# The rest of the folded queries made by TensorE and taken by ScalarE, the folded pieces ahead of the scores

## The reference

```python
q_c_lat = _linear(x, d_q_w, d_q_b); kv_c = _linear(x, d_kv_w, d_kv_b)
q_c = _linear(q_c_lat, u_q_w, u_q_b); k_c = _linear(kv_c, u_k_w, u_k_b)
q_r, k_r = _rope(_linear(q_c_lat, qr_w, qr_b)), _rope(_linear(kv_c, qr_w, qr_b))
q, k = concatenate([q_c, q_r]), concatenate([k_c, k_r])
scores = einsum('bhqd,bhkd->bhqk', q, k) / sqrt(192)
ctx = einsum('bhqk,bhkd->bqhd', softmax(scores), v)
out = _linear(ctx, out_w, out_b)
```

## Time and profile before

| | us |
|---|---|
| median of 3 runs | 2483.41 |
| lowest and highest | 2482.87, 2486.58 |
| profiled execution, span from first to last instruction | 2481.1 |
| TensorE busy | 2204.9 (89%) |
| VectorE busy | 2144.0 (86%) |
| ScalarE busy | 1862.6 (75%) |
| GpSimd busy | 1073.9 (43%) |

### The profile page before, as it was taken

How to read it: one execution, slowest core, us unless ns; L and a number is a source line. 1 busy time by engine, 2 the same in 40 slices (tenths; PEclk the granted TensorE clock), 3 DMA queues, 4 the chain that set the end, 5 groups by cost and what they waited for, 6 DMA issues and landing times.

```text
span 2481.1 us, 50682 instructions
## 1 busy us (share of the span) xinstructions
PE 2204.9 (89%) x18456; PEld 1581.5 (64%) x18544; DVE 2144.0 (86%) x3182; ACT 1862.6 (75%) x2640; POOL 1073.9 (43%) x1480
## 2 busy tenths in 40 slices
PE   4888888869997889999999999999999999988899
PEld 2444444445554567777777777767767777766687
DVE  6888888768896999999999999999999999988522
ACT  4877777747675688888888888888888888877411
POOL 3312112102223575666656656656656656622200
PEclk9999999979998899999999999999999999999899
DMA  3000000050000599999999999999999999999100
GB/s 128 1 2 2 2 2 2 1 115 1 1 1 1 92 182 191 197 188 188 197 190 194 192 192 193 192 189 191 196 191 190 193 194 192 205 192 193 41 17 17
DMA packets 1119318, 300.69 MB, mean 121 GB/s; under 512 B 1107232, under 2 KB 1116416, under 8 KB 1118208
## 3 DMA queue, kind: packets, MB, share of 16 engines
q1 hardware_dynamic: 1116224, 295.21, 68.7%
q10 hardware_dynamic: 2848, 2.23, 0.3%
HBM read 18.45 MB, written 2.10 MB: 8 GB/s over the span
## 4 chain that ended last, share of the span: by engine, by line
DVE 28%; PE 21%; issue 9%; ACT 4%; DMA 4%; SPq 0%; DVEq 0%; ACTq 0%
DVE parts L1651 13%; DVE lows L1635 12%; DMA partsT<-parts 4%; PE psS L1586 3%; PE psOb L1506 3%; PE psS L1489 2%; PE psS L1491 2%; PE psS L1490 2%; ACT parts L1835 2%; PE psOb L1542 1%; PE psOb L1507 1%; ACT prob L1825 1%; PE psOb L1606 1%; PE psPb L1606 1%; DVE rden L1661 1%
## 5 line engine op out<-in xcount | busy, mean ns | idle before, releaser
L1825 ACT ACTIVATE prob<-psS,shift 128x1024 f32<-128x1024 f32 x512 | 574.4, 1122 | 171.0 <-DVE shift L1643 161.2
L1651 DVE TENSOR_TENSOR parts<-prob,parts 128x1024 f16<-128x1024 f32 x512 | 661.0, 1291 | 20.8 <-ACT parts L1835 17.3
L1635 DVE TENSOR_REDUCE lows<-psS 128x1 f32<-128x1024 f32 x512 | 621.9, 1215 | 4.9 <-PE psS L1491 4.7
L1835 ACT CAST parts<-prob 128x1024 f16<-128x1024 f32 x512 | 536.7, 1048 | 21.2 <-DMA partsT<-parts 17.4
L1489 PE MATMUL psS<-k_hi,q_lo 128*128 128x512 f32 x1024 | 449.8, 439 | 100.3 <-ACT prob L1825 93.4
L1506 PEld LDWEIGHTS psOb<-kv,partsT 128*128 128x128 f16 x4096 | 356.7, 97 | 92.1 <-issue 75.7
L1506 PE MATMUL psOb<-kv,partsT 128*128 128x130 f16 x4096 | 396.3, 221 | 13.9 <-DMA partsT<-parts 13.8
L1490 PE MATMUL psS<-k_lo,q_hi 128*128 128x512 f32 x1024 | 407.1, 398 | 0.0
L1491 PE MATMUL psS<-k_hi,q_hi 128*128 128x512 f32 x1024 | 406.9, 397 | 0.0
L1507 PE MATMUL psOb<-kv,partsT 128*128 128x66 f16 x4096 | 386.3, 192 | 0.0
L1507 PEld LDWEIGHTS psOb<-kv,partsT 128*128 128x128 f16 x4096 | 360.1, 98 | 1.0 <-issue 1.0
(11 more groups left out here) (298 smaller groups left out, 4024.2 us busy)
## 6 DMA issues: line engine op xcount, KB each, us to landing
partsT<-parts SPq DMA_TRANSPOSE x512, 4.8
ef<-in_ewT SPq DMA_DIRECT2D x1, 2048.0 KB, 11.1
rf<-in_rwT SPq DMA_DIRECT2D x1, 2048.0 KB, 10.4
outw_s<-in_outwT SPq DMA_DIRECT2D x1, 2048.0 KB, 8.6
trig<-in_trig SPq DMA_DIRECT2D x2, 1024.0 KB, 11.2
out_x<-ot SPq DMA_DIRECT2D x16, 128.0 KB, 1.7
wug<-in_wupT SPq DMA_DIRECT2D x4, 256.0 KB, 3.9
wug<-in_wgateT SPq DMA_DIRECT2D x4, 256.0 KB, 3.7
```

What stands on the lines that cost most here:

```text
L1635: dve.tensor_reduce(lows[:, n % 2, g:g + 1], psS[:, (2 * n + g) % 3, :], AX_X, ALU.min).then_inc(half_min, 1)
L1651: dve.tensor_tensor(parts[:, s, 1, :], prob[:, g, :], parts[:, s, 0, :], ALU.subtract).then_inc(low_done, 1)
L1825: act.activation(prob[:, g, :], psS[:, (2 * n + g) % 3, :], ACT.Exp, bias=shift[:, n % 2:n % 2 + 1], scale=-1.0).then_inc(exp_done, 1)
L1835: act.copy(parts[:, s, 0, :], prob[:, g, :]).then_inc(high_done, 1)
```

## The change

- A tile `negative` of 128x128 in float32r: its latent rows hold minus the identity in the latent columns and zero in the rotary columns. VectorE makes it with two instructions ahead of the first rotation and counts `negated`; TensorE waits for that once, ahead of the loop.
- For heads 1 to 15, VectorE's `rest` goes. Instead TensorE, behind the contexts of the same iteration, waits for `folded` and adds `negative^T q_hi` to the bank psP (`lessen`), counting `lessened`; ScalarE, in the next iteration behind `exponential(n,0)` and ahead of `normalise(n-3)`, waits for `lessened` and writes `q_lo = psP + beta_h` (the new `rest`, counting `rested`).
- TensorE makes the folded piece (piece mod 3 is 2) ahead of `scores(n+1,0)`. The other pieces stay behind the scores.
- Nothing changes for head 0's pieces, for the other engines' orders, or in the waits of `project`.

```diff
--- before.py
+++ after.py
@@ -1330,11 +1330,13 @@
         part = sb(L, "part", [P, D])
         lows = sb(L, "lows", [P, 2, 2])
         shift = sb(L, "shift", [P, 2])
+        negative = sb(L, "negative", [P, P], F32R)
 
         piece_ready, rotated, added_up = sem("b_piece"), sem("b_rotated"), sem("b_added_up")
         round_done, rests_done = sem("b_round"), sem("b_rests")
         keys_summed, keys_rested = sem("b_keys_summed"), sem("b_keys_rested")
         folded, rested = sem("b_folded"), sem("b_rested")
+        negated, lessened = sem("b_negated"), sem("b_lessened")
         score_ready, half_min, shift_ready, exp_done = sem("b_score"), sem("b_half_min"), sem("b_shift"), sem("b_exp")
         high_done, low_done = sem("b_high"), sem("b_low")
         landed = [sem(f"b_landed{s}") for s in range(RING)]
@@ -1461,6 +1463,12 @@
                     pe.matmul(bank, fl2, lat_hi[0:C, cols], start=True, stop=False)
                     pe.matmul(bank, fh2, lat_lo[0:C, cols], start=False, stop=False)
                     pe.matmul(bank, fh2, lat_hi[0:C, cols], start=False, stop=True).then_inc(piece_ready, 1)
+
+            def lessen(head, piece):
+                j = piece // 3
+                pe.wait_ge(folded, 4 * head + j + 1)
+                pe.matmul(psP[:, :], negative[latent, :], q_hi[latent, q_slot(head, j), :], start=False, stop=True,
+                          skip_group_check=True).then_inc(lessened, 1)
 
             def scores(n, g):
                 if n >= TILES:
@@ -1548,13 +1556,19 @@
                 project(0, piece)
             scores(0, 0)
             scores(0, 1)
+            pe.wait_ge(negated, 1)
             for n in range(TILES + 2):
+                piece = piece_at(n) if n < TILES else None
+                if piece is not None and piece % 3 == 2:
+                    project(n // NT + 1, piece)
                 scores(n + 1, 0)
                 scores(n + 1, 1)
-                if n < TILES and piece_at(n) is not None:
-                    project(n // NT + 1, piece_at(n))
+                if piece is not None and piece % 3 < 2:
+                    project(n // NT + 1, piece)
                 context(n - 2, 0)
                 context(n - 2, 1)
+                if piece is not None and piece % 3 == 2:
+                    lessen(n // NT + 1, piece)
                 output(n - LATER)
                 for i in units_at.get(n, ()):
                     spread(i)
@@ -1719,6 +1733,8 @@
                                   ALU.subtract).then_inc(keys_rested, 1)
                 dve.wait_ge(keys_rested, j + 1)
 
+            dve.tensor_scalar(negative[latent, rotary], ident[latent, rotary], 0.0, None, ALU.mult)
+            dve.tensor_scalar(negative[latent, latent], ident[latent, latent], -1.0, None, ALU.mult).then_inc(negated, 1)
             for j in range(NB):
                 rotate(0, 3 * j)
                 rotate(0, 3 * j + 1)
@@ -1735,8 +1751,8 @@
                 low(n, 0)
                 half(n + 1, 1)
                 whole_min(n + 1)
-                if n < TILES and piece_at(n) is not None:
-                    (rotate, rotate, rest)[piece_at(n) % 3](n // NT + 1, piece_at(n))
+                if n < TILES and piece_at(n) is not None and piece_at(n) % 3 < 2:
+                    rotate(n // NT + 1, piece_at(n))
                 invert(n - 2)
                 if n == TILES - 4:
                     scale_signs()
@@ -1802,6 +1818,11 @@
                 act.activation(q_hi[latent, slot, :], piece_bank(head, piece)[latent, :], ACT.Identity,
                                bias=beta_h[latent, 0:1]).then_inc(folded, 1)
 
+            def rest(head, piece):
+                slot = q_slot(head, piece // 3)
+                act.wait_ge(lessened, 4 * (head - 1) + piece // 3 + 1)
+                act.activation(q_lo[latent, slot, :], psP[latent, :], ACT.Identity, bias=beta_h[latent, 0:1]).then_inc(rested, 1)
+
             def round_queries(head, j, halves_scored):
                 act.wait_ge(added_up, sums(head, j) + 1)
                 if halves_scored:
@@ -1878,6 +1899,8 @@
             for n in range(TILES + 3):
                 ahead = n < TILES and n // NT + 1 < NH
                 exponential(n, 0)
+                if 0 < n <= TILES and piece_at(n - 1) is not None and piece_at(n - 1) % 3 == 2:
+                    rest((n - 1) // NT + 1, piece_at(n - 1))
                 normalise(n - 3)
                 take_output(n - LATER - 1)
                 high(n, 0)
```

## The result

| | before | after |
|---|---|---|
| median, us | 2484.72 (4 runs, 2482.87 to 2486.58) | 2569.22 (4 runs, 2567.43 to 2572.24) |
| ratio, 95% interval | | 1.034 (1.0328 to 1.0353) |
| span of the profiled execution, us | 2481.1 | 2570.9 |

The change makes the kernel 3.4% slower, some 85 us. The direction and the main mechanism were forecast, the size was not: +45 us, with an upper end of +75. This is a wrong prediction of the size.

The account below looks back on a forecast made before the run. It took the fixed engine orders in each tile as the limit, with VectorE full where it does a rotation. Losses of 20.8 and 17.9 us, 7.2 for meetings, less 1, gave +45 us: 2528.5 us, range 2510 to 2558.

Parts of the forecast that it names:

- part 3: Folded piece ahead of the scores: TensorE waits for VectorE's rotation, so `half(n+1,0)` comes 1.27 us late, 1.33 with a take.
- a rival of 0.11: Slower by much more: long GpSimd meetings, a late ScalarE rest or a 1.2 GHz TensorE clock; about 2575 us, chance 0.11.
- part 1: Rest leaves VectorE for ScalarE, whose step costs 0.60 us: the rest's period gains 0.62 us without a take, 0.68 with one.
- without a take: Tiles where ScalarE does no `take_output`, 32 of the 60 rest periods: net loss 0.65 us each, 20.8 us.
- meetings: VectorE and GpSimd instructions that overlap and slow each other: 0.12 us in each of 60 places, 7.2 us.
- With a take: Tiles where ScalarE does `take_output`, 28 of the 60 rest periods: net loss 0.64 us each, 17.9 us.
- parts 1 and 4: Part 1 has its own line; the other: VectorE's `low` against GpSimd additions, 0.12 us each, bounds 0 and 0.5.
- the ring: VectorE-ScalarE loop from `shift` through exponential, `normalise`, `high`, `low`, `half` to `shift`: 5.59 us without a take, 5.94 with one.
- the wait for `rotated`: Sign: TensorE idles before the first folded matmul in 60 places, about 1.4 us without outputs and 0.8 with.
- the extra matmul: One more 64-row matmul behind the contexts, 60 times: 14 us of TensorE, hidden; ScalarE doesn't wait for it.
- VectorE's idle time released by scores: Sign: VectorE idles about 1.3 us ahead of the first `half` behind each folded piece, some 78 us in total.
- The rival that took VectorE's load for the limit: Faster: VectorE's load is what counts and the stall is under 0.6 us; 2471 us, chance 0.05.

Follow-up runs that it names:

- Run 3: Changed kernel plus four filler matmuls ahead of each folded piece where TensorE has no output to make: 2560.54 us, 1.0305 of the kernel before.
- run 7: Changed kernel with the folded piece between the two halves of scores and ScalarE's rest moved behind `high(n,0)`: 2470.54 us, 0.9949 of the kernel before.
- run 6: Changed kernel with the folded piece between the halves of scores and ScalarE's rest a plain copy without bias: rest periods without a take 5.72 us instead of 5.89.
- run 5: Changed kernel with GpSimd's addition of the output to x cut from 256 columns to 8: 2552.78 us in a single execution.
- run 8: Changed kernel with the folded piece between the halves of scores and GpSimd's second addition, `whole_k`, one step later: 2471.70 us, 0.9958 of the kernel before.
- run 1: Changed kernel with the folded piece back behind both halves of the scores: 2476.17 us, 0.9967 of the kernel before.

## Why the prediction was wrong in size

- **The stall (part 3) was right in place and mechanism and 0.21 us too small.** Forecast 1.27 and 1.33 us late; the tile shown is late by 1626.88 - (1623.36 + 1.99) = 1.53, the 1.99 being the distance in the earlier trace rows (1572.33 less 1570.47, plus 0.13). Terms: rotation to TensorE 0.10 instead of 0.04; where the folded matmuls give way to the scores two spacings are long, 0.32 (1624.87 to 1625.19) and 0.33 (1625.19 to 1625.52), where I had used 0.233. The earlier trace rows had a hint: it is 0.33 from the scores to the folded piece at 1499.44. I averaged over the spacings within one kind of matmul and forgot the change of kind. Over all 60, (103.3 - 12.8) / 60 = 1.51 us against the 1.30 of my sum: 12.5 us of the 40 missing.
- **The granted clock, 12.8 us.** I had it as part of a rival of 0.11, at 1.2 GHz altogether. It happened in 15 of the 60 stalled periods, in each for part of the period, and the sum had no term for it. Run 3 shows it.
- **ScalarE's step (part 1) costs 0.84 to 0.85 us, not 0.60, outside my bounds of 0.57 to 0.71.** The bounds counted the step's own length and missed that the exponential ahead of it loses its overlap too: 1.14 us from start to start (1630.66 to 1631.80) instead of 1.01. In the earlier trace rows the fold had waited 0.16 us for its piece, so its front could not show this. It is felt in the 32 periods without a take: 5.71 us forecast (5.59 and 0.12 for meetings), 189.8 / 32 = 5.93 measured, 32 x 0.22 = 7 us.
- **With a take the period was not VectorE's to give back (parts 1 and 4).** Part 1 let the 6.62 us fall to the ring, 5.94, with 0.12 for meetings: 6.06. It measured 6.60: 28 x 0.54 = 15 us. I took the 6.62 for VectorE's load, but the earlier trace rows already had `low` ending 1.09 us after GpSimd's addition, and the addition kept its place, 4.35 us after the `shift`. I had seen the 1.71 us `low` and called it a meeting that is partly in the 6.62; it was what ended the period. The periods stayed at 6.60 with the rest on ScalarE's ring, off it (run 7) and shorter (run 6); only the short addition (run 5) or GpSimd's other order (run 8) brought them down.
  In the tiles with a take, and in 9 of the 32 others, I also had the order of `whole_k` and `low(n,1)` the wrong way round: the addition came first and `low` took 2.17 to 2.29 us. That cost 0.2 to 0.3 us in four places and next to nothing elsewhere (runs 5 and 8).
  The Trainium skill (SBUF — State Buffer, section Who interferes with whom) says that a VectorE instruction with two SBUF inputs contends with a GpSimd instruction that reads SBUF, that the lock on the shared ports is exclusive, and that issue order decides who blocks. Here the trace agrees to 0.13 us: the `low` at 1630.90 ended at 1633.08, 1.08 us after the end of the addition that had begun at 1630.71 and took 1.29; alone `low` takes 1.21.
- **Together.** 12.5 + 12.8 + 7 + 15 is 47 on top of 45, and the periods behind and the others are 2 us shorter in sum: the 90 us by which the spans differ. The medians differ by 85; the other executions had less time at the lower clock (0.975 on average against 0.971).
- **What held:** the wait for `rotated`, where it is felt (TensorE idles 0.63 to 0.87 us with outputs and mostly 1.29 without; I had said 0.8 and 1.4), VectorE's idle time released by scores, the extra matmul, for which ScalarE's rest never waits (no idle time ahead of any of its 60 instructions), ScalarE 45 us busier (1907.4), the gain from the moved rest smaller than the stall. The rival that took VectorE's load for the limit fell: the stall is 1.5 us, where it needed less than 0.6, and by run 1 the load that went is worth 9 us.

## What to carry to other kernels

Before work moves forward in an engine's order, look at who last read the buffer that it overwrites: a wait that was never felt in the old place becomes the engine's order in the new one, and everything queued behind it is late. Moving it one step instead of two, behind the first half of the scores, kept all of the use and none of the wait. And a step moved off a full engine onto another is priced by where it stands on the ring between the two, with the overlap it takes from its neighbours, not by either engine's total. Check also, for each kind of tile, whether a third engine ends the period: here GpSimd did in 28 of the 60, and nothing taken off VectorE there could be felt.

## What the runs showed of the hardware

- Pauses of 1.3 us on TensorE, with dense work around them, went ahead of a granted clock of 1.2 GHz for about 3 us: in 15 of the 32 places whose pause is 1.28 us or more, and in none of the 28 whose pause is 0.63 to 0.87. With four matmuls in the pause it happened in 1 of the 32. What parts the 15 from the other 17 was not found.
- Neighbouring ScalarE steps that start at the same partition overlapped by about 0.1 us (1578 of 1697 pairs with less than 0.06 us between them, in the trace after); steps that start at different partitions never did (0 of 318). For a step on partitions 64 to 127 between two that start at 0 that is 0.84 us in all, 0.68 of it its own, with a bias, and 0.74 as a copy.
- `low` ended 1.08 to 1.09 us after the GpSimd addition that it met, in all 28 tiles of both traces, though it started 0.06 us later in the changed kernel (3.80 us after the `shift` instead of 3.74).
- Behind matmuls with weights of 64 rows the next one with 128 rows started 0.32 us later instead of 0.23, and the one behind it 0.33 us later.
